# A cross-network tower: the first group in blocks, weights split from PSUM, tiles dealt out anew

## What is computed

```python
e = stack([tbl_f[ids[:, f]] for f in range(39)], axis=1)        # b, 39, 16
x0 = xk = e
for idx, (W, b) in enumerate(((w0, b0), (w1, b1), (w2, b2))):   # W: 39, k, 128
    z = relu(einsum('bhd,bkd,hks->bsd', x0, xk, W) + b[None, :, None])
    if idx != 2:
        xk = z[:, :64, :]; direct.append(z[:, 64:, :])
    else:
        direct.append(z)
z = sum(concatenate(direct, axis=1), axis=-1)                   # b, 256
h = concatenate([z, dense_ctx], axis=1)                         # b, 272
h = maximum(h @ W_top1 + b_top1, 0)                             # 512
h = maximum(h @ W_top2 + b_top2, 0)                             # 256
y = h @ W_top3                                                  # b, 1
```

## Time and profile before

| | |
|---|---|
| median of 3 runs | 2657.89 us (2656.21 to 2662.3) |
| profiled execution | 2672.21 us, span 2670.4 us |
| PE busy | 2437.1 us, 91% |
| DVE busy | 2314.0 us, 87% |
| POOL busy | 1869.5 us, 70% |
| ACT busy | 1127.6 us, 42% |
| transfers | 469.80 MB, mean 176 GB/s |

### The profile page before, as it was taken

How to read it: one execution, slowest core, us unless ns; L and a number is a source line. 1 busy time by engine, 2 the same in 40 slices (tenths; PEclk the granted TensorE clock), 3 DMA queues, 4 the chain that set the end, 5 groups by cost and what they waited for, 6 DMA issues and landing times. The chain is left out here.

```text
span 2670.4 us, 31273 instructions
## 1 busy us (share of the span) xinstructions
PE 2437.1 (91%) x7862; PEld 1466.0 (55%) x7862; DVE 2314.0 (87%) x1839; ACT 1127.6 (42%) x1109; POOL 1869.5 (70%) x1122
## 2 busy tenths in 40 slices
PE   0389999999999999999999999999999999999978
PEld 0145555555555555555565555555555555555556
DVE  1369899999998999989999999999899899999982
ACT  0034344444444444444444444444444444444435
POOL 6268777787868778786877878786877778555430
PEclk9899999999999999999999999999999999999999
DMA  3788888888888888887899887888898788888710
GB/s 61 159 188 178 192 197 193 190 182 188 177 187 190 202 198 179 193 185 174 179 204 208 183 184 176 191 182 191 193 201 186 166 191 180 187 197 196 175 46 9
DMA packets 184309, 469.80 MB, mean 176 GB/s; under 512 B 37746, under 2 KB 74211, under 8 KB 184275
## 3 DMA queue, kind: packets, MB, share of 16 engines
q1 hardware_dynamic: 160941, 461.79, 76.0%
q0 software_dynamic: 19968, 5.15, 2.1%
q10 hardware_dynamic: 3367, 2.48, 0.4%
HBM read 456.96 MB, written 12.33 MB: 176 GB/s over the span
## 5 line engine op out<-in xcount | busy, mean ns | idle before, releaser
L547 POOL TENSOR_TENSOR low<-prod,high 128x1024 fp32r<-128x1024 f32 x448 | 1088.3, 2435 | 520.7 <-ACT high L636 514.8
L525 POOL DMA_INDIRECT landed<-in_tbl,rows_id x624 | 772.9, 1239 | 178.0 <-issue 165.4
L777 DVE TENSOR_TENSOR prod<-spread,maps 128x2048 f32<-128x2048 f32 x352 | 798.3, 2283 | 94.4 <-PE zacc_a L924 31.6
L636 ACT ACTIVATE high<-prod 128x1024 fp32r<-128x1024 f32 (+1 forms) x544 | 572.3, 1058 | 618.0 <-DVE prod L777 483.6
L889 PE MATMUL zacc_a<-prod,w_plain 128*128 128x512 f32 (+2 forms) x1408 | 657.4, 597 | 52.1 <-DVE prod L762 51.9
L889 PE MATMUL zacc_b<-prod,w_plain 128*128 128x512 f32 (+2 forms) x1408 | 657.5, 597 | 3.2 <-DVE prod L781 2.2
L781 DVE TENSOR_TENSOR prod<-spread,maps 128x1024 f32<-128x1024 f32 x320 | 379.7, 1213 | 54.3 <-DMA spread<-x_periods 52.0
L889 PEld LDWEIGHTS zacc_a<-prod,w_plain 128*128 128x128 f32 (+2 forms) x1408 | 267.7, 191 | 285.0 <-issue 245.4
L889 PEld LDWEIGHTS zacc_b<-prod,w_plain 128*128 128x128 f32 (+2 forms) x1408 | 268.4, 191 | 233.3 <-issue 201.4
L889 PE MATMUL zacc_b<-high,w_low 128*128 128x512 f32 x736 | 278.4, 459 | 27.5 <-ACT high L636 25.0
L924 PE MATMUL zacc_b<-low,w_high 128*128 128x512 f32 x736 | 282.2, 465 | 18.1 <-POOL low L547 15.6
(11 more groups left out here) (109 smaller groups left out, 1843.6 us busy)
## 6 DMA issues: line engine op xcount, KB each, us to landing
spread<-x_periods SPq DMA_DIRECT2D x608, 512.0 KB
shifted<-x_periods SPq DMA_DIRECT2D x640, 156.0 KB
x_thrice<-x_periods SPq DMA_DIRECT2D x96, 156.0 KB
landed<-in_tbl,rows_id POOLq DMA_INDIRECT x624
x_periods<-x SPq DMA_DIRECT2D x32, 256.0 KB
spread<-x_periods SPq DMA_DIRECT2D x32, 256.0 KB
features<-feat ACTq DMA_DIRECT2D x16, 128.0 KB
spread<-features SPq DMA_DIRECT2D x4, 512.0 KB, 5.2
```

The lines of the kernel that those rows point to most:

```text
L525: nc.gpsimd.indirect_dma_start(out=landed[:, f, :], out_offset=None, in_=tables[f], in_offset=bass.IndirectOffsetOnAxis(ap=rows_id[:, f:f ...
L547: nc.gpsimd.tensor_tensor(low[0:rows, at_, :], prod[0:rows, at_, :], high[0:rows, slot(j, SPLIT, NH), :], ALU.subtract).then_inc(s_lowp, 1)
L636: nc.scalar.activation(high[0:rows, h, :], made(turn, j)[0:rows, :], ACT.Copy).then_inc(s_round, 1)
L777: nc.vector.tensor_tensor(prod[:, at_:at_ + 2, :], spread[:, t:t + 2, :], maps[:, :].unsqueeze(1).to_broadcast([128, 2, COLS]), ALU.mult). ...
```

## The change

- `PLAN` is dealt out anew: F 22 to 24 tiles, P 14 to 12, D 8 to 5, V 3 to 6 (two of them the half-height ones, as before). By the slots, doubles go from 11 to 14 in a turn. `NH` 5 to 4.
- The activations stand at other places of ScalarE's order: layer 0 behind the round of tile 29's place instead of 30's, layer 1 two tiles earlier; the channel sums at tile 27 instead of 26 (layers 0 and 1) and at 14 of the next turn instead of 21 (layer 2). On VectorE a V low part is written ahead of a D low part that falls on the same tile.
- First group: 39 gathers in five blocks with a semaphore each (8 fields, the last 7); every block is transposed, copied and written by itself. SP's queue holds a third of the w0 loads, the first block's write, four spread loads (two pieces), the second third, and so on. Six of ten pieces are loaded before the squares' loads, which stay ahead of the other four. Staging begins at tile 13 of `spread`.
- Weights: ScalarE copies each staged tile to PSUM and to `w_high` (or `w_plain`); VectorE subtracts PSUM and `w_high` into `w_low`. The copy of x's blocks is put between these casts.
- End: the top weights are loaded after tile 34 of the last turn, three quarters of the features after tile 38; ScalarE casts (place 41), GpSimd clears and subtracts, TensorE transposes half of the dense inputs at place 42 and half after the last tile.

```diff
-PLAN = "PFPFPFPFDPFDPFDPFDVV" "FFFFFFF" "PFPFPFPFDPFDPFDPFDFV"
+PLAN = "FVFPPPFPFFDPFDVFFPFV" "FFFFFFF" "FPFFFVPFDPVFDPPDFPFV"
-NP, NH = 8, 5
+NP, NH = 8, 4
-LZ = 4
+RELU0_AT, RELU1_AT, RELU2_AT = N1 + N0 - 1 + 3, N1 - 1 + 2, 3
-SUM01_AT, SUM2_AT = N1 + LZ + 2, N1 + 1
+SUM01_AT, SUM2_AT = 27, 14
-FIRST_PIECES = 2
+EARLY_BLOCKS = 3
+STAGE_AT = 13
+TOP_TILES, FEATS_TILES = 8, 12
+CAST_AT, TURN_TOP_AT = 41, 42
...
+            def write_block(q):
+                rows = min(128, FLAT - 128 * q)
+                if q < TURNED - 1:
+                    sp.wait_ge(s_first_x, q + 1)
+                else:
+                    sp.wait_ge(s_x, 1)
+                for k in range(PERIODS):
+                    sp.dma_start(x_periods[0, k, 128 * q:128 * q + rows, :], x[0:rows, q, :]).then_inc(s_first_w, 16)
+            third = -(-len(W0_RUNS) // EARLY_BLOCKS)
+            for q in range(TURNED):
+                load_w0(W0_RUNS[third * q:third * (q + 1)])
+                write_block(q)
+                if q < EARLY_BLOCKS:
+                    sp.wait_ge(s_first_w, 16 * PERIODS * (q + 1))
+                    for piece in (2 * q, 2 * q + 1):
+                        load_spread(Turn(None, 0), piece)
...
                 if turn.fixed and turn.number() == -1 and j == 0:
-                    write_x(nxt)
                     load_first(nxt)
-                    sp.wait_ge(s_prep, 1)
-                    for q in range(FIRST_PIECES):
-                        load_spread(nxt, q)
...
                 if turn.fixed and turn.number() == -1 and j == SQUARED[-1]:
-                    for q in range(FIRST_PIECES, PIECES):
+                    sp.wait_ge(s_prep, 1)
+                    for q in range(2 * EARLY_BLOCKS, PIECES):
                         load_spread(nxt, q)
...
+                if turn.fixed and turn.number() == CHUNKS - 1:
+                    if j == LAST[TOP_TILES - 1] + 1:
+                        sp.wait_ge(s_prod, n_prod(turn, LAST[TOP_TILES - 1]) + 1)
+                        load_top()
+                    if j == LAST[FEATS_TILES - 1] + 1:
+                        sp.wait_ge(s_prod, n_prod(turn, LAST[FEATS_TILES - 1]) + 1)
+                        for n in range(3):
+                            load_features(n)
...
+            act.wait_ge(s_wload12, 16 * 4)
+            cast_weights([j for j in early_tiles if j in PAIRED])
+            copy_block(1)
+            cast_weights([j for j in early_tiles if j in LAST])
+            copy_block(2)
+            copy_block(3)
+            act.wait_ge(s_fold, 2)
+            cast_weights(late_tiles)
+            copy_block(4)
...
+                if turn.fixed and turn.number() == CHUNKS - 1 and j == CAST_AT:
+                    cast_top()
+                if turn.fixed and turn.number() == CHUNKS and j == 0:
+                    high_features(0)
+                    copy_dense(0)
...
-                    nc.vector.tensor_tensor(w_low[0:rows_of(j), rank(j, SPLIT), :], staged_tile(j),
-                                            w_high[0:rows_of(j), rank(j, SPLIT), :], ALU.subtract)
+                        nc.vector.tensor_tensor(w_low[0:rows, rank(j, SPLIT), :], weight_home(j)[0:rows, :],
+                                                w_high[0:rows, rank(j, SPLIT), :], ALU.subtract)
...
-                for kind, behind in (("D", SUB_D), ("V", SUB)):
+                for kind, behind in (("V", SUB), ("D", SUB_D)):
```

More of the change, by code:

```diff
@@ L243, in build @@
         s_fold = sem("s_fold")
+        s_cast = sem("s_cast")
         s_first = sem("s_first")
+        s_first_g = [sem(f"s_first_g{q}") for q in range(TURNED)]
+        s_first_t = sem("s_first_t")
+        s_first_x = sem("s_first_x")
+        s_first_w = sem("s_first_w")
         s_all = sem("s_all")
@@ L275, in build @@
         s_top = sem("s_top")
+        s_cast_top = sem("s_cast_top")
+        s_wc = sem("s_wc")
         s_fh = sem("s_fh")
@@ L399, in build, with staged_tile, weight_home, first_bank @@
         block = ctx.enter_context(nc.Block())
+        def staged_tile(j):
+            rows = rows_of(j)
+            return (st1[0:rows, j, :] if j in PAIRED else st0a[0:rows, j - N1, :] if j in SQUARED
+                    else st2[0:rows, j - N1 - N0, :])
+        later_split = [j for j in [*PAIRED, *LAST] if PLAN[j] != "F"][24:]
+        early_tiles = [j for j in [*PAIRED, *LAST] if j not in later_split]
+        late_tiles = [*SQUARED, *later_split]
+        def weight_home(j):
+            tiles = early_tiles if j in early_tiles else late_tiles
+            r = [i for i in tiles if PLAN[i] != "F"].index(j)
+            return [*zacc, maps1][r // 8][:, r % 8 * MAPS:(r % 8 + 1) * MAPS]
+        def first_bank(q):
+            return q % 2 * BANK
         def w0_run(start, n):
@@ L521, in _, with gather @@
             nc.gpsimd.memset(mark[:, :], 0.0).then_inc(s_mark, 1)
-            def gather(first, last):
+            def gather(first, last, of=None):
                 for f in range(first, last):
@@ new lines, in _, with cast_weights @@
+            copy_block(0)
+            load_w0(W0_RUNS[middle:])
+            def cast_weights(tiles):
+                for j in tiles:
+                    rows = rows_of(j)
+                    if PLAN[j] == "F":
+                        last = nc.scalar.activation(w_plain[0:rows, rank(j, "F"), :], staged_tile(j), ACT.Copy)
+                        continue
+                    nc.scalar.activation(weight_home(j)[0:rows, :], staged_tile(j), ACT.Copy)
+                    if stacked(j):
+                        nc.scalar.activation(w_high[HALF:128, rank(j, SPLIT), :], staged_tile(j), ACT.Copy)
+                    last = nc.scalar.activation(w_high[0:rows, rank(j, SPLIT), :], staged_tile(j), ACT.Copy)
+                last.then_inc(s_cast, 1)
@@ L754, in product @@
                 if PLAN[j] == "D" and j not in FIRST_D:
-                    dve.wait_ge(s_lowv, n_kind(turn, j, ON_DVE))
+                    dve.wait_ge(s_lowv, n_kind(turn, max(i for i in range(j) if PLAN[i] == "D"), ON_DVE) + 1)
                 if j in SQUARED:
@@ L925, in contract_low, with turn_block, turn_first, turn_dense @@
                 return done
+            def turn_block(q, at_):
+                rows = min(128, FLAT - q * 128)
+                flat = landed[:, :, :].rearrange("p f d -> p (f d)")
+                return nc.tensor.transpose(maps2[0:rows, at_:at_ + ROWS], flat[:, q * 128:q * 128 + rows],
+                                           ident[:, :])
+            def turn_first():
+                for q in range(TURNED):
+                    pe.wait_ge(s_first_g[q], 16 * len(BLOCKS[q]))
+                    if q > 1:
+                        pe.wait_ge(s_first_x, q - 1)
+                    turn_block(q, first_bank(q)).then_inc(s_first_t if q < TURNED - 1 else s_turned, 1)
+            def turn_dense(i):
+                if i == 0:
+                    pe.wait_ge(s_mlp, 16 * MLP_LOADS)
+                for n in (2 * i, 2 * i + 1):
+                    for g in range(PER):
+                        done = nc.tensor.matmul(
+                            sides[i][0:DENSE, n % 2 * BANK + g * ROWS:n % 2 * BANK + (g + 1) * ROWS],
+                            m_dense[:, PER * n + g, :], m_ident, start=g == 0, stop=g == PER - 1, skip_group_check=True)
+                done.then_inc(s_dense, 1)
             def turn_x(n):
-                pe.wait_ge(s_gather, n.group(16 * FIELDS, 16 * FIELDS))
+                pe.wait_ge(s_gather, n.group(16 * FIELDS, 0))
                 if not n.fixed or n.number() > 2:
```

243 lines of the change are left out of this document (129 added, 114 removed).

## The result

| | before | after |
|---|---|---|
| median | 2660.1 us (2656.21 to 2666.53, 4 runs) | 2547.99 us (2541.7 to 2555.95, 4 runs) |
| ratio | | 0.9578, 95% interval 0.9537 to 0.9618 |
| span of the profiled execution | 2670.4 us | 2540.3 us |
| PE busy | 2437.1 us, 91% | 2418.3 us, 95% |
| DVE busy | 2314.0 us, 87% | 2255.7 us, 89% |

The forecast was 2553 us, with turns of 74.0. The three rows at the foot of the table differ by 32.3, 79.7 and 18.0 us, 130 in all. That is 18 more than the medians differ (112), and the start is where the excess lies, as the experiments show.

The account below looks back on a forecast made before the run. Spread loads plus VectorE's tail were taken to set the 76.46 us turn, TensorE 4 us below. Gains of 76 (turns), 15 (start) and 14 (end) sum to 105: profile 2567, median 2553 us, range 2505 to 2620.

Parts of the forecast that it names:

- -15, -76 and -14 (-105): Forecast gains in us at the start, over 31 turns (2.46 each), and at the end.
- the 15.3 us behind the piece of 16 and 17: VectorE's work from that spread piece's landing to the end of the next squares: 15.3 us, against 18.8 before.
- the same bytes, so again 57.7: Transfers from the squares' end until the piece of tiles 16 and 17 lands: 57.7 us, unchanged.
- Limits that nearly meet: Per turn: TensorE's work 73.1, the loop of transfers plus VectorE's tail 73.0, and VectorE's lead at the last layer close.
- VectorE's lead at the start of the last layer: VectorE starts the last layer some 5 us before TensorE; low parts want 4.1 of that, so 1 us is spare.
- the allowance above the sums, 1.0 us: Turns taken as 74.0 with three limits at 73, because none hides the others' unevenness; bounds 73.1 and 76.0.
- The wait at tile 31: TensorE's wait before 1345.41, tile 31's rounding standing behind three activations on ScalarE; the activations' new place was to remove it.
- the sum of layer 2: Channel sum in VectorE's tail behind tiles 16 and 17; its leaving was part of the fall from 18.8 to 15.3 us.
- The reason given for choosing among the bounds: At the start, SP's issues and VectorE's splits are slow together, SP's release unproven: -15 us, nearer the slow end.
- The layer's begin at 95 or 131: Paired layer's begin, by SP's rate for w0 loads: near 131 at 1.25 us each, near 95 at 0.36 or 0.49.
- the 14.3 us between profile and median: Median 2657.89 lies 14.3 us below the profiled 2672.21; the forecast took the same off 2567 to reach 2553.
- Rival 2: V low parts, both inputs in SBUF, lock against GpSimd's low parts: up to +5 us a turn, about 2785; 9%, centred on 2690.

Follow-up runs that it names:

- turns_only: Kernel before with only the new plan, ring, places and order of low parts, start and end as before: 2623.29 us, ratio 0.9795, turns of 75.00.
- old_places: Changed kernel with only the old places of the activations and channel sums: 2562.51 us, ratio 0.9563, turns of 74.04.
- the next step: Changed kernel with square loads issued behind all spread pieces, and tiles 9 and 38 turned from F to P: 2585.35 us, ratio 0.9664.

## Why the prediction held, point by point

- **The time.** 2553 us forecast, 2548 measured; turns 74.0 and 73.98. That the turns agree to 0.02 is luck, as the next two points show. Measured in one job, the terms are -16.5, -73.0 and -17.3 (-106.8) beside -15, -76 and -14 (-105). The latter count 31 turns, the former 30, with the last turn's part in the end.
- **The turns: right total, two errors that in part cancel.** The step that failed is the 15.3 us behind the piece of 16 and 17. It left out that the last squares wait for their own loads once the work between them is gone, 1.0 to 1.2 us a turn; 17.1 were measured. So the plan alone gives turns of 75.0, a gain of 1.6 to 1.8 and not 2.46. The other error is "the same bytes, so again 57.7": the bytes are the same but their packets got 2% faster through addresses or semaphore numbers, 0.85 us a turn. Had the declarations fallen as in `turns_only`, the forecast would have been 1.0 us by 31 turns, about 30 us, too low, still within its range.
- **Limits that nearly meet.** Two of the three are shown: moving the loads gives 73.09, taking work off TensorE gives nothing, both together give 71.70. The third, VectorE's lead at the start of the last layer, no run tests. TensorE's own work is 72.7 and not 73.1, and the loop 56.4 + 17.1 = 73.5 and not 73.0; the allowance above the sums, 1.0 us, was an estimate without a row, and it covered what was left.
- **Places.** The wait at tile 31 was to go and the sum of layer 2 to leave the tail. Both happen, but the first comes of the plan (tile 31 is F now), and the new places are worth nothing, as `old_places` shows: what they move is not late in the loop that sets the turn.
- **The start.** -15 forecast, -16.5 measured where both kernels have the slow issues. The reason given for choosing among the bounds did not hold: SP's rate is not set by VectorE's splits, nor by its queue, so that the value near the slow end fits is luck. The layer's begin at 95 or 131, which I made to hang on the kernel, hangs on the execution: the first paired product came at 99.0 and 116.6 in two profiles of one kernel. Even with the slow issues this was 11 earlier than before (127.5) and not 5 later, since they ended at 57 and did not last over all loads. SP's first eight loads, which the prediction gives as 0.49 each, took 5.27 us, 0.66 each; only its fast bound rests on that.
- **The base.** I took the 14.3 us between profile and median as something that profiles have. That profile had the slow start, the profile after had not (2542.07, against a median of 2547.99), and the 18 us that this costs are the gap between 130 for the profiles and 112 for the medians. As two medians of one kernel differ by 16 to 20 us with the start, this is the likely reason; the starts of the executions without a profile are not known.
- **The end.** -14 forecast; the last squares to the end took 17 to 18 us less, some 2 of which are the last turn's part, so about 16. The gap went from 17.1 to 3.6, and the 2.6 us of slow top matmuls came back.
- **Locks.** The full V low parts took 1288 ns, the D ones 1217; the stacked ones fell from 1857 to 1242 (64 of them, 1.2 us a turn), so in this plan they hardly meet GpSimd. Rival 2 was rightly small here, and its lock is part of what stopped the next step.

## What to carry to other kernels

Where several limits lie within 1 us, test them in pairs: an edit that is worth nothing alone was worth 39 us with the other one. In a queue that refills buffers, put first what is wanted first and last what is wanted last. Look at single turns before a mean is taken for a sum: here one long turn in 30 hid that TensorE's work is 0.4 us less than thought. And compare profiles by stages that both show: a start that differs by 18 us from one execution to the next is otherwise booked as a gain.

## What the hardware showed that was not expected

- Between 20 us and 57 to 94 us of some executions SP's and ScalarE's issues and VectorE's instructions mostly stand 0.70 or 1.40 us apart, with pauses of 9 to 12 us and short bursts at the usual pace, while GpSimd's gathers beside them (until 51 us) keep their 1.25. All kernels of one job have it or none. Its cause is open.
- Eight bytes of SBUF and nine semaphores that nobody uses changed the mean 4 KB packet from 288.4 to 282.6 ns and the kernel by 1%.
